# Four fp32 products over 392 columns made in three fp32r terms; the input splits shared out over ScalarE and GpSimd

## The chip, the cores and the metric

The kernel runs on one core of one Trainium2 chip. The metric is the time of one execution in device microseconds (us). Below this stands one time for each run, and one execution was also recorded by the hardware profiler.

Engines are named as the profile names them: PE is TensorE (its weight loads are PEld), DVE is VectorE, ACT is ScalarE, POOL is GpSimd, SP is SyncE, which issues the transfers. PSUM is the memory that the products write, in eight banks of 2 KB per partition; SBUF is the memory that all engines work from.

## The reference

Four attention blocks are applied in turn to 64 images of 256 channels and 14 x 14 = 196 tokens, all in float32.

```python
# block 0 (convolutional attention)
out = batchnorm1(x)
q, k, v = split(W_qkv_pw @ depthwise3x3(out))       # k, v resized to 7 x 7
o = softmax((q k^T + bias) * s) v                   # 4 heads
out = W_out_pw @ depthwise3x3(o) + x
x = W_mlp @ relu(batchnorm2(out)) + out
# block 1 (linear attention)
xn = group_norm(x, 8 groups);  k = softmax_channels(k);  q = softmax_tokens(q)
x = proj((q (k^T v))) + xn
# block 2 (8 heads)
hid = group_norm(x, 32 groups);  a = softmax(q k^T) v;  x = x + proj(a)
# block 3 (1 head)
xn = group_norm(x, 32 groups);   x = x + W_o (softmax(q k^T / 16) v)
```

## The kernel before

Images go through in 32 pairs. A pair's tensor has 128 partitions, 2 channel halves (c = 0, 1) and 392 columns (two images of 196 tokens). All four blocks of a pair stay on the chip; about five pairs are under way at once, each at another stage.

The order of the work is written out by hand in tables of numbers, one for each engine (PE_AT, ACT_AT, DVE_AT, POOL_AT, SP_AT). An entry such as `"kv0": 297` puts the piece kv0 of a pair in place 297 mod 128 of a loop body that has 128 places, 297 // 128 = 2 turns after the pair came in. One turn of the loop body (a period below) therefore does each piece once, for several pairs. Every engine works through its own list in order; semaphores tell it when inputs are there and when a buffer is free. A wait at the head of an engine's list holds all that stands behind it.

Names of pieces: q0, k0, v0, s0, t0, o0 are block 0's queries, keys, values, scores, transposes, output of attention; pw its second pointwise product (after the depthwise convolution conv2), mlp its last product; kv, q1, ctx, out belong to block 1; hq, hk, hv, sc, tn, av, rt, rep, proj to block 2 (sc scores, tn transposes, av values' products, rt and rep the denominators spread over the heads, proj the projection); v3, q3, s3, t3, o3 to block 3. gn1, gn2, gn3 are the group norms' products over groups.

A group norm goes like this: DVE takes statistics, PE averages over a group (a product over 8 columns), DVE copies the result (`gn_group`), GpSimd works out scale and shift in 20 small instructions on 4 elements (`normalized`, L561 to L585, with three Newton steps), and then writes the normalized input itself in 4 instructions over 196 columns (L590).

Products are of two kinds. `product` (L1168) multiplies in fp32: a product of 128 x 392 over 256 channels shows as 4 MATMUL records. `split_product` (L1174) takes inputs and weights that were split into two fp32r parts, high and low, and adds three terms (high x high, high x low, low x high) for each channel half: 6 records. For blocks 1, 2 and 3 the split of the normalized input is done each time by one ACT cast (the high part, L778) and one DVE subtraction (the low part, L1092) for each channel half, in buffers xs1, xs2, xs3. q0, pw, mlp and proj, two pieces each, are fp32 products of 392 columns.

The four banks ps_a, ps_b, ps_c, ps_e take turns by the table BANK_USES; the four banks of ps_s hold block 2's scores, their transposes, and the av products.

The depthwise convolutions are 2 + 16 DVE instructions each: k = 0 is a TENSOR_SCALAR for each half, k = 1 to 8 are SCALAR_TENSOR_TENSOR (`y = window * tap + y`, two inputs from SBUF), L1139 and L1158.

## Time and profile before

| | us |
|---|---|
| time, median of 3 runs | 2169.32 (2168.65 to 2169.71) |
| the profiled execution's own time | 2170.37 |
| its span, first to last instruction | 2168.3 |

| engine | busy us | share of the span | instructions |
|---|---|---|---|
| PE | 2076.3 | 96% | 15232 |
| PEld | 1686.7 | 78% | 15232 |
| DVE | 1820.4 | 84% | 4359 |
| ACT | 1527.8 | 70% | 5172 |
| POOL | 1278.3 | 59% | 2954 |

The busy time is that in which at least one instruction of the engine runs. ACT's instructions overlap, so the distance between two starts is less than a duration; the same holds for PE's, whose ends are modelled. The chain of waits that ended last lies on PE for 91% of the span, on DVE for 3%, on POOL for 2%.

### The profile page before, as it was taken

The page shows a single profiled execution, that of the slowest core. Times are in us where ns is not written, and L with a number is a line of the kernel's source. Part 1 is how long each engine was busy: PE and PEld are TensorE (multiplying, and loading weights), DVE is VectorE, ACT ScalarE, POOL GpSimd, SP SyncE. Part 2 cuts the span into 40 slices and gives each one's busy share as a digit, 9 for nine tenths or more (in the row PEclk, how much of TensorE's full clock was granted, in tenths as well). Part 3 has the DMA queues.
Part 4 walks back from the last instruction along what each step waited for, and adds up shares of the span by engine and source line. Part 5 has one row for each costly group of instructions (what it writes and reads, how often), then busy time and mean ns, then how long its engine had stood idle before and what let it go on. Part 6 is the DMA issues. An engine that isn't in the chain of part 4 may idle for free.

```text
span 2168.3 us, 58678 instructions
## 1 busy us (share of the span) xinstructions
PE 2076.3 (96%) x15232; PEld 1686.7 (78%) x15232; DVE 1820.4 (84%) x4359; ACT 1527.8 (70%) x5172; POOL 1278.3 (59%) x2954
## 2 busy tenths in 40 slices
PE   4679999999999999999999999999999999999987
PEld 3466888888888788888878888887888888788775
DVE  6778899988888998988899898888989888887532
ACT  2256777777777777777777777777777777777763
POOL 2455666666666666666666666666666666664311
PEclk8799999999999999999999999999999999999977
DMA  3000011001101100110110011011101100100000
GB/s 126 15 23 23 16 39 39 29 23 37 37 22 37 37 30 22 37 37 22 37 37 30 22 37 37 23 36 37 37 15 37 37 31 28 38 31 24 24 23 23
DMA packets 29828, 70.22 MB, mean 32 GB/s; under 512 B 6261, under 2 KB 7105, under 8 KB 29761
## 3 DMA queue, kind: packets, MB, share of 16 engines
q1 hardware_dynamic: 26928, 67.68, 9.0%
q10 hardware_dynamic: 2832, 1.73, 0.3%
q8 instruction: 32, 0.52, 0.1%
q14 instruction: 36, 0.29, 0.0%
HBM read 30.86 MB, written 12.85 MB: 20 GB/s over the span
## 4 chain that ended last, share of the span: by engine, by line
PE 91%; DVE 3%; POOL 2%; issue 2%; ACT 1%; SPq 1%; DMA 0%; POOLq 0%; DVEq 0%; ACTq 0%
PE ps_c L1166 19%; PE ps_a L1166 17%; PE ps_e L1166 17%; PE ps_b L1166 17%; PE ps_s L1166 10%; PE ps_s L1216 8%; POOL gn_t L579 1%; PE ps_a L1292 1%; DVE y L1158 1%; PE ps_e L1454 0%; PE ps_e L1292 0%; PE ps_b L1454 0%; PE ps_e L1399 0%; SPq L475 0%; ACT e L827 0%
## 5 line engine op out<-in xcount | busy, mean ns | idle before, releaser
L827 ACT ACTIVATE e<-ps_s,nm 98x196 f32<-98x196 f32 x1024 | 426.1, 446 | 89.9 <-DVE nm L956 89.8
L590 POOL TENSOR_SCALAR xn<-x,gn_scale,gn_shift 128x196 f32<-128x196 f32 x384 | 353.2, 933 | 20.8 <-POOL gn_shift L585 20.8
L1158 DVE SCALAR_TENSOR_TENSOR y<-opad,w_dw,y 128x406 f32<-128x406 f32 x512 | 301.8, 645 | 0.0
L1139 DVE SCALAR_TENSOR_TENSOR y<-xpad,w_dw,y 128x406 f32<-128x406 f32 x512 | 300.8, 640 | 0.0
L956 DVE TENSOR_REDUCE nm<-ps_s 98x4 f32<-98x784 f32 x256 | 240.6, 962 | 41.8 <-PE ps_s L1166 41.8
L834 ACT COPY pt<-ps_s 98x392 f32<-98x392 f32 x512 | 229.1, 503 | 42.6 <-PE ps_s L1216 41.8
L568 POOL TENSOR_TENSOR gn_t<-gn_group 128x4 f32<-128x4 f32 x96 | 34.3, 358 | 372.9 <-DVE gn_group L1006 286.5
L827 ACT ACTIVATION_READ_ACCUMULATOR e<-ps_s,nm 98x1 f32 x1024 | 231.6, 226 | 0.0
L1216 PE MATMUL ps_s<-w_eye,e 98*98 98x98 f32 x2048 | 204.6, 251 | 0.6 <-ACT e L827 0.6
L1216 PEld LDWEIGHTS ps_s<-w_eye,e 98*98 98x98 f32 x2048 | 186.3, 131 | 24.1 <-issue 16.2
L581 POOL TENSOR_SCALAR gn_t<-gn_t 128x4 f32<-128x4 f32 x288 | 119.7, 416 | 58.6 <-POOL gn_t L579 58.6
L1092 DVE TENSOR_TENSOR xs<-xn,xs 128x392 fp32r<-128x392 f32 x192 | 113.1, 589 | 41.7 <-ACT xs L778 39.3
L1166 PE MATMUL ps_a<-xs,ws_q 128*128 128x392 f32 x576 | 131.5, 363 | 0.4 <-ACT v L807 0.4
L1166 PE MATMUL ps_s<-k,q 32*98 32x196 f32 x2048 | 121.3, 352 | 8.6 <-ACT a L841 6.8
L778 ACT CAST xs<-xn 128x392 fp32r<-128x392 f32 x192 | 106.3, 554 | 31.4 <-POOL xn L590 31.3
L841 ACT COPY a<-ps_s 128x196 f32<-128x196 f32 x128 | 41.9, 327 | 119.2 <-PE ps_s L1166 113.5
L1166 PE MATMUL ps_s<-pt,v 98*32 98x196 f32 x2048 | 113.5, 339 | 3.5 <-ACT pt L834 2.7
L1166 PEld LDWEIGHTS ps_a<-xs,ws_q 128*128 128x128 f32 x576 | 102.0, 188 | 16.8 <-issue 7.7
L1166 PEld LDWEIGHTS ps_s<-k,q 32*98 32x98 f32 x2048 | 78.3, 163 | 46.8 <-issue 36.8
L937 DVE BATCH_NORM_STATS2 gn_stats<-x 128x6 f32<-128x196 f32 x384 | 110.4, 350 | 1.5
L579 POOL TENSOR_TENSOR gn_t<-gn_t,gn_half 128x4 f32<-128x4 f32 x288 | 95.7, 332 | 22.6
L578 POOL TENSOR_TENSOR gn_t<-gn_y 128x4 f32<-128x4 f32 x288 | 87.5, 304 | 23.1
(245 smaller groups left out, 5596.8 us busy)
## 6 DMA issues: line engine op xcount, KB each, us to landing
x_in<-in_x SPq DMA_DIRECT2D x32, 392.0 KB, 3.1
x_res<-in_x SPq DMA_DIRECT2D x32, 392.0 KB, 3.3
x2b<-x SPq DMA_DIRECT2D x32, 392.0 KB, 2.6
out<-x SPq DMA_DIRECT2D x32, 392.0 KB, 2.6
out_pairs<-out SPq DMA_DIRECT2D x32, 392.0 KB, 3.5
w_q<-in_q SPq DMA_DIRECT2D x3, 256.0 KB
w_k<-in_k SPq DMA_DIRECT2D x3, 256.0 KB
w_v<-in_v SPq DMA_DIRECT2D x3, 256.0 KB
```

The lines of the kernel that those rows point to most:

```text
L579: link(g.tensor_tensor(t.t[:], t.t[:], t.half[:], ALU.mult))
L581: link(g.tensor_scalar(t.t[:], t.t[:], 1.5, None, ALU.add))
L590: g.tensor_scalar(dst[:, c, of_image(i)], src[:, c, of_image(i)], t.scale[:, j:j + 1], t.shift[:, j:j + 1], ALU.mult, ALU.add).then_inc(t. ...
L827: s.activation(e2[:, j, tc], tile(use)[0:HALF, of_image(tc)], ACT.Exp, bias=nm2[:, j, tc:tc + 1], accum_out=den2[:, 2 * i + tc, h:h + 1]). ...
L834: s.copy(turned(j), tile(use)[0:HALF, 0:N2]).then_inc(emptied(use), 1)
L937: v.bn_stats(t.stats[:, j], src[:, j // 2, of_image(j % 2)]).then_inc(t.stat_steps.sem, 1)
L956: v.tensor_reduce(out=nm2[:, two], in_=ps_s[0:HALF, two, 0:N2].rearrange("p b (c n) -> p b c n", c=2), axis=AX.X, op=ALU.max, negate=True) ...
L1092: v.tensor_tensor(dst[:, 1, c], src[:, c], dst[:, 0, c], ALU.subtract).then_inc(gn[n].low.sem, 1)
L1139: v.scalar_tensor_tensor(out=dst, in0=window(xpad, c, k, CR), scalar=tap, in1=dst, op0=ALU.mult, op1=ALU.add).then_inc(conv1_steps.sem, 1)
L1158: v.scalar_tensor_tensor(out=dst, in0=window(opad, c, k, CR), scalar=tap, in1=dst, op0=ALU.mult, op1=ALU.add).then_inc(conv2_steps.sem, 1)
L1166: return nc.tensor.matmul(dst, lhsT, rhs, start=start, stop=stop)
L1216: last = nc.tensor.transpose(tile(use)[0:HALF, of_tile(sc, tc)], e2[:, j, tc, sc * HALF:(sc + 1) * HALF], eye[0:HALF, 0:HALF])
```

## The change

- q0, pw, mlp and proj become `split_product`s: 6 records in place of 4 for each of the 8 pieces of a pair. Their weights are split once at the start.
- Their inputs are split each time, for each channel half by an ACT cast and a GpSimd subtraction: y1 (for q0) and an2 (for proj) into a buffer xs_a, y2 (for pw) and act0 (for mlp) into a buffer xs_b. xs_a also takes the place of rt2, act0 now lies in y2's memory, an2 in a2's.
- The normalized input of the three group norms is written by ACT (4 instructions of 128 x 196 each), no longer by GpSimd.
- The low parts for blocks 1, 2 and 3 are subtracted by GpSimd, no longer by DVE.
- The av products go to ps_a and ps_e and ps_c, out of ps_s.
- All tables of order and BANK_USES are new, and what PE folds of the weights at the start is spread over the first pair's stages.

```diff
 POOL_AT = {
-    "resize0": 0, "resize1": 16, "probs0": 64, "probs1": 96, "gn1": 240, "gn2": 304, "gn3": 544, "rows3": 592,
+    "resize0": 87, "y1_low0": 93, "y1_low1": 98, "resize1": 104, "probs0": 168, "probs1": 180, "y2_low0": 244,
...
-                for c in range(KC):
-                    for i in range(2):
-                        j = 2 * c + i
-                        alone()
-                        g.tensor_scalar(dst[:, c, of_image(i)], src[:, c, of_image(i)], t.scale[:, j:j + 1],
-                                        t.shift[:, j:j + 1], ALU.mult, ALU.add).then_inc(t.done.sem, 1)
...
+                    for n, src, dst, _ in splits:
+                        for c in range(KC):
+                            p = pair_of(t, u, POOL_AT[f"low{n}_{c}"])
+                            if p is not None:
+
+                                pool.wait_ge(gn[n].high.sem, gn[n].high.at(p, c + 1))
+                                g.tensor_tensor(dst[:, 1, c], src[:, c], dst[:, 0, c], ALU.subtract).then_inc(gn[n].low.sem, 1)
+
+                    for c in range(KC):
+                        p = pair_of(t, u, POOL_AT[f"y1_low{c}"])
+                        if p is not None:
+                            pool.wait_ge(y1_cast.sem, y1_cast.at(p, c + 1))
+                            g.tensor_tensor(by_image(xs_a[:, 1, c]), conv_tokens(y1, c), by_image(xs_a[:, 0, c]),
+                                            ALU.subtract).then_inc(y1_cut.sem, 1)
...
+                    for n, src, dst in ((1, x1, xn1), (2, x2, xn2), (3, x3, xn3)):
+                        for c in range(KC):
+                            p = pair_of(t, u, ACT_AT[f"norm{n}_{c}"])
+                            if p is not None:
+                                act.wait_ge(gn[n].steps.sem, gn[n].steps.at(p + 1, 0))
+                                if n == 1 and has_before(p):
+                                    act.wait_ge(*read(p - 1, f"out{c}"))
...
+                                for i in range(2):
+                                    j = 2 * c + i
+                                    s.activation(dst[:, c, of_image(i)], src[:, c, of_image(i)], ACT.Identity,
+                                                 scale=gn[n].scale[:, j:j + 1], bias=gn[n].shift[:, j:j + 1]
+                                                 ).then_inc(gn[n].done.sem, 1)
...
+                            act.wait_ge(*read(p, f"rep{c}"))
+                            act.wait_ge(*full(p, latest("rep0", "rep1")))
+                            s.copy(by_image(xs_a[:, 0, c]), an2[:, :, c]).then_inc(an2_cast.sem, 1)
...
-                            for source in elsewhere(use, "rep0", "rep1"):
-                                pe.wait_ge(*read(p, source))
-                            product(tile(use)[:, 0:N2], lambda k: w["p2"][:, k, of_chunk(c)], lambda k: an2[:, :, k]
-                                    ).then_inc(filled(use), 1)
-
+                            pe.wait_ge(an2_cut.sem, an2_cut.at(p, KC))
+                            split_product(tile(use)[:, 0:N2], lambda a, k: ws["p2"][:, a, k, of_chunk(c)],
+                                          lambda b, k: xs_a[:, b, k]).then_inc(filled(use), 1)
```

Three places in the new order matter for what follows. The first is GpSimd behind block 1's group norm (the piece gn1), before the change:

```order
L584 TENSOR_TENSOR gn_t<-gn_group,gn_scale 128x4
L585 TENSOR_TENSOR gn_shift<-w_gn_b,gn_t 128x4
L590 TENSOR_SCALAR xn<-x,gn_scale,gn_shift 128x196 x4
L547 TENSOR_TENSOR rs_d<-y 128x168
L548 TENSOR_TENSOR rs_d<-rs_d,w_frac 128x168
```

And the same place after it:

```order
L618 TENSOR_TENSOR gn_t<-gn_group,gn_scale 128x4
L619 TENSOR_TENSOR gn_shift<-w_gn_b,gn_t 128x4
L687 TENSOR_TENSOR xs_a<-a,xs_a 128x392 x2
L664 TENSOR_TENSOR xs<-xn,xs 128x392 x2
L581 TENSOR_TENSOR rs_d<-y 128x168
```

The four instructions on xn are gone; in their place stand the low parts of proj's input and of block 1's input, four subtractions that each wait for a cast by ACT.

The second place is DVE behind the copy of the same group norm's result (`gn_group`). The y rows are block 0's first convolution, nm the score maxima of block 2, m, t, nm (98x2) those of block 3. Before the change:

```order
L1006 COPY gn_group<-ps_b 128x8
L1063 TENSOR_TENSOR rt<-ps_e,rt 8x392
L1139 SCALAR_TENSOR_TENSOR y<-xpad,w_dw,y 128x406 x2
L956 TENSOR_REDUCE nm<-ps_s 98x4 x2
L1139 SCALAR_TENSOR_TENSOR y<-xpad,w_dw,y 128x406 x2
L1103 TENSOR_REDUCE m<-ps_e 98x2
L1105 TENSOR_TENSOR t<-m,rb 98x2
L1106 SCALAR_TENSOR_TENSOR nm<-t,rs 98x2
L1139 SCALAR_TENSOR_TENSOR y<-xpad,w_dw,y 128x406 x4
```

After it:

```order
L1104 COPY gn_group<-ps_e 128x8
L1221 SCALAR_TENSOR_TENSOR y<-xpad,w_dw,y 128x406 x2
L1158 TENSOR_TENSOR xs_a<-ps_a,xs_a 8x392
L1054 TENSOR_REDUCE nm<-ps_s 98x4 x2
L1186 TENSOR_REDUCE m<-ps_a 98x2
L1188 TENSOR_TENSOR t<-m,rb 98x2
L1189 SCALAR_TENSOR_TENSOR nm<-t,rs 98x2
L1221 SCALAR_TENSOR_TENSOR y<-xpad,w_dw,y 128x406 x8
L1166 TENSOR_TENSOR a<-ps_e,a 128x2x196
L1221 SCALAR_TENSOR_TENSOR y<-xpad,w_dw,y 128x406 x2
```

The convolution's instructions stood in groups of 2, 2 and 4; now eight stand in a row, while GpSimd works on this group norm.

The third place is ACT around the casts for block 1 (`xs`). opad is block 0's attention output, a that of block 2. Before the change:

```order
L834 COPY pt<-ps_s 98x392 x2
L778 CAST xs<-xn 128x392
L725 COPY opad<-ps_b 128x14x14 x2
L788 ACTIVATE q<-ps_a,qb2s 128x392
L778 CAST xs<-xn 128x392
L725 COPY opad<-ps_c 128x14x14 x2
```

After it:

```order
L932 COPY pt<-ps_s 98x392 x2
L871 CAST xs_a<-a 128x392
L840 ACTIVATE xn<-x,gn_shift,gn_scale 128x196 x4
L879 CAST xs<-xn 128x392
L780 COPY opad<-ps_b 128x14x14 x2
L879 CAST xs<-xn 128x392
L780 COPY opad<-ps_c 128x14x14 x2
```

ACT now waits here for GpSimd's scale and shift before four instructions on xn, and the copies to opad, from which conv2 starts, stand behind them.

## Rows read from the trace of the kernel before

**Rows 1.** Stretches: busy us (count) of each engine, clock, DMA share, GB/s

```profile
600.00:1230.60 630.60, 629.90 (x4741) 515.18 (x4740) 565.69 (x1350) 473.29 (x1611) 405.85 (x921) 1.00 0.09 32
240.00:2020.00 1780.00, 1777.59 (x13401) 1455.04 (x13395) 1580.02 (x3781) 1335.45 (x4545) 1133.09 (x2594) 1.00 0.09 32
```

**Rows 2.** Timeline of PE: start us, us, line, operation, out<-in, records merged

```profile
1001.11 1.24 PE L1166 MATMUL ps_a<-xs,ws_q 128*128 128x392 f32 x6
1002.18 1.48 PE L1166 MATMUL ps_c<-act,w_mlp 128*128 128x392 f32 x4
1003.50 1.48 PE L1166 MATMUL ps_b<-act,w_mlp 128*128 128x392 f32 x4
...
1010.24 0.28 PE L1166 MATMUL ps_b<-gn_mine,w_group 128*128 128x8 f32 x2
...
1022.04 1.35 PE L1166 MATMUL ps_a<-xs,ws_q 128*128 128x392 f32 x6
1023.23 0.82 PE L1166 MATMUL ps_b<-pt,v 128*128 128x196 f32 x4
...
1026.77 1.58 PE L1166 MATMUL ps_b<-an,w_p 128*128 128x392 f32 x4
1028.28 0.92 PE L1166 MATMUL ps_s<-k,q 32*98 32x196 f32 x16
1029.13 1.62 PE L1166 MATMUL ps_c<-ws_kv,xs 128*98 128x512 f32 x6
...
1632.82 1.48 PE L1166 MATMUL ps_c<-act,w_mlp 128*128 128x392 f32 x4
```

**Rows 3.** Timeline of ACT, same columns

```profile
1027.56 1.15 ACT L875 ACTIVATE e<-e,r 98x196 f32<-98x196 f32 x3
...
1056.22 0.54 ACT L778 CAST xs<-xn 128x392 fp32r<-128x392 f32 x1
1056.63 0.75 ACT L673 ACTIVATE xpad<-x_in,bn_shift,bn_scale 128x392 f32<-128x392 f32 x1
```

**Rows 4.** Groups by line: busy us, mean ns, idle before and releaser

```profile
L1092 DVE TENSOR_TENSOR xs<-xn,xs 128x392 fp32r<-128x392 f32 x192 | 113.1, 589 | 41.7 <-ACT xs L778 39.3
L590 POOL TENSOR_SCALAR xn<-x,gn_scale,gn_shift 128x196 f32<-128x196 f32 x384 | 353.2, 933 | 20.8 <-POOL gn_shift L585 20.8
```

**Rows 5.** POOL's instructions on tile p: duration ns min/median/max

```profile
L602 POOL TENSOR_TENSOR p<-s,r x64: 840/846/1182, 47.2 to 1954.6; 98x392 f32<-98x392 f32 x64
```

**Rows 6.** Waits of POOL from 600 to 1230.6 us: total, times, longest

```profile
POOL gn_t L568 <- DVE gn_group L1006: 91.7, 30, 4.7
POOL rb L615 <- ACT v3t L850: 34.6, 10, 3.5
...
POOL p L602 <- DVE r L979: 4.1, 10, 0.4
```

**Rows 7.** Timeline of DVE: convolution steps in a row

```profile
137.68 5.60 DVE L1139 SCALAR_TENSOR_TENSOR y<-xpad,w_dw,y 128x406 f32<-128x406 f32 x10
...
1045.85 4.50 DVE L1158 SCALAR_TENSOR_TENSOR y<-opad,w_dw,y 128x406 f32<-128x406 f32 x8
...
1080.09 2.30 DVE L1139 SCALAR_TENSOR_TENSOR y<-xpad,w_dw,y 128x406 f32<-128x406 f32 x4
```

**Rows 8.** Timeline of POOL in the same places, and one group norm at the end

```profile
137.10 6.24 POOL L579 TENSOR_TENSOR gn_t<-gn_t,gn_half 128x4 f32<-128x4 f32 x1
...
1045.22 5.51 POOL L590 TENSOR_SCALAR xn<-x,gn_scale,gn_shift 128x196 f32<-128x196 f32 x1 [0.22 <-POOL gn_shift L585]
...
1080.89 0.45 POOL L582 TENSOR_TENSOR gn_y<-gn_y,gn_t 128x4 f32<-128x4 f32 x1
...
2090.72 0.20 POOL L568 TENSOR_TENSOR gn_t<-gn_group 128x4 f32<-128x4 f32 x1 [22.78 <-PE ps_c L1166]
...
2097.28 1.98 POOL L590 TENSOR_SCALAR xn<-x,gn_scale,gn_shift 128x196 f32<-128x196 f32 x4 [0.22 <-POOL gn_shift L585]
```

**Rows 9.** Waits of ACT from 600 to 1230.6 us: total, times, longest

```profile
ACT a L841 <- PE ps_s L1166: 35.6, 20, 3.2
```

**Rows 10.** Timeline of PE in the first pair's stages

```profile
67.12 2.95 PE L1166 MATMUL ps_e<-y,w_o 128*128 128x392 f32 x4 [8.70 <-DVE y L1158]
```

More of the change, by code:

```diff
@@ L320, in latest, with earliest, ahead @@
             return max(names, key=filled_at)
+        def earliest(*names):
+            return min(names, key=filled_at)
+        def ahead(use, other):
+            return (PE_AT[use] - 1 - PE_AT[other]) // SLOTS
         def comes_after(use, older):
@@ new lines, in step @@
+                    for c in range(KC):
+                        p = pair_of(t, u, ACT_AT[f"y1_high{c}"])
+                        if p is not None:
+                            act.wait_ge(conv1_steps.sem, conv1_steps.at(p, KC * 8 + c + 1))
+                            older = p + ahead(earliest("q0_0", "q0_1"), latest("proj0", "proj1"))
+                            if exists(older):
+                                act.wait_ge(*full(older, latest("proj0", "proj1")))
+                            if has_before(p):
+                                act.wait_ge(*full(p - 1, latest("q0_0", "q0_1")))
+                            s.copy(by_image(xs_a[:, 0, c]), conv_tokens(y1, c)).then_inc(y1_cast.sem, 1)
@@ new lines, in step @@
+                    for c in range(KC):
+                        p = pair_of(t, u, ACT_AT[f"y2_high{c}"])
+                        if p is not None:
+                            act.wait_ge(conv2_steps.sem, conv2_steps.at(p, KC * 8 + c + 1))
+                            if has_before(p):
+                                act.wait_ge(*full(p - 1, latest("mlp0", "mlp1")))
+                            s.copy(by_image(xs_b[:, 0, c]), conv_tokens(y2, c)).then_inc(y2_cast.sem, 1)
+                    for c in range(KC):
+                        p = pair_of(t, u, ACT_AT[f"act0_high{c}"])
+                        if p is not None:
+                            act.wait_ge(act0_done.sem, act0_done.at(p, c + 1))
+                            act.wait_ge(*full(p, latest("pw0", "pw1")))
+                            s.copy(xs_b[:, 0, c], act0[:, c]).then_inc(act0_cast.sem, 1)
```

213 lines of the change are left out of this document (133 added, 80 removed), and 69 rows, old and new, of tables (ACT_AT, BANK_USES, DVE_AT, PE_AT).

## The prediction, made before the changed kernel ran

> **What bounds the kernel now.** I read the busy time by stretch first. From 240 to 2020 us PE is busy 1777.6 of 1780 us at a granted clock of 1.00 [rows 1]: 2.4 us of idle time in 1780. So between these marks the time is what PE's records take one after the other, and the other engines matter only when one holds PE up. The same mlp piece starts at 1002.18 and, ten periods on, at 1632.82 [rows 2], so a period is 63.06 us, and the stretch holds 28.2 of them. Per period (630.6 us is ten) DVE is busy 56.6, ACT 47.3, POOL 40.6 us [rows 1]. POOL's figure is too small: most of its instructions wait for the one ahead on POOL itself. Its waits for others are 9.2 + 3.5 + 0.4 = 13.0 us a period [rows 6], so 50.0 of 63.06 are taken. The remaining 390 us, filling and draining, have PE partly idle, as in the 8.70 us before pw of the first pair [rows 10].
>
> **PE.** Distances from start to start count, not durations. An fp32 piece over 392 columns takes 1003.50 - 1002.18 = 1.32 us, and 1.51 us at the costlier place (1026.77 to 1028.28); three terms take 1.07 (1001.11 to 1002.18) to 1.19 us (1022.04 to 1023.23) [rows 2]. As most fp32 pieces are at 1.32 and few above, I take 1.34 against 1.10: 0.24 a piece, times 8 = 1.9 us a period. Bounds: 8 x (1.32 - 1.19) = 1.0, and 2.3 if the fp32r pieces are all at 1.07 and two fp32 pieces at about 1.5. PE alone then needs 63.06 - 1.9 = 61.15 us. The av products keep their form; another bank changes no PE time, and only frees the first score bank earlier. The wider weights are split at the start, beside the fp32 folding that now leaves PE's front.
>
> **ACT.** Added: 8 casts, whose distance is 0.41 us (1056.22 to 1056.63), 3.3 us; and 12 instructions of 196 columns from SBUF. The nearest is e<-e,r, three in 1.15 us with a last one of about 0.45: 0.35 each, 4.2 us [rows 3]. ACT gets 47.3 + 7.5 = 54.8 us of 61.2. This hides beside PE if ACT's forced waits stay under 6.4 us; before, it had 15.7 us to spare, most of it harmless waiting ahead of PE (the largest, for av, 3.6 us a period [rows 9]).
>
> **DVE.** Six subtractions go, 6 x 0.589 = 3.5 us [rows 4]: 53.1 us. None was waited for by PE, so nothing comes from it but room.
>
> **POOL.** Twelve instructions on xn go: 353.2 / 32 = 11.0 us a period [rows 4]. Fourteen subtractions over 392 columns come. The only one of this size on POOL takes 0.846 us, 1.182 at most [rows 5]: 14 x 0.85 = 11.9 us, at most 16.5. 50.0 - 11.0 + 11.9 = 50.9 us of 61.2. That looks free, but the 0.93 us mean of the removed ones [rows 4] tells of something else: alone they take 0.5 (four in 1.98 us, [rows 8]), and one took 5.51 us. It lies under eight convolution steps of DVE in a row (1045.85, 4.50 us); an instruction of four elements took 6.24 us under ten (137.68, 5.60 us); under four steps at 1080.09 one took 0.45 us [rows 7, 8]. So POOL, when caught at the start of such a row, stands until the row ends, and DVE is not slowed (0.55 us a step each time).
>
> The Trainium skill, SBUF — State Buffer, on engine ports, calls the shared pair an exclusive lock that goes to whichever of the two engines starts first, the loser being fully blocked. Full blocking agrees with the 5.51 us; that the first one wins does not, as POOL's instruction started at 1045.22, before DVE's row. What it would make of the time is the last rival.
>
> The new order puts eight steps in a row on DVE just when POOL works on gn1, and leaves eight in a row under gn3. Where the blocked work used to be xn of a norm that had time, it now lies inside a chain that PE waits for. Between gn1's product and kv0, PE now has about 18.9 us of other work (1010.24 to 1029.13, [rows 2]), and by the same distances about 17.7 us for the 19 pieces that stand there after the change. The chain in that gap: DVE copy 0.3, POOL's 20 instructions 6.55 (2090.72 to 2097.28, [rows 8]), four xn on ACT 1.4, cast 0.4, opad copies 0.4, cast 0.4, last subtraction 0.85: 10.3 us undisturbed. Fully blocked by all 14 steps in that stretch, 14 x 0.55 = 7.7, it is 18.0 us and kv0 is late by some 0.3, or by 1.1 if a subtraction is at its 1.18 and the an2 pair is in its way: about 0.7. If POOL slips in between the steps, nothing is late. gn3, followed by y2's subtractions and pw, has the same form: 0 to 0.7. Bounds 0 to 1.35 a period; two of the three rows of steps above blocked POOL fully, but chains have to be wholly blocked to be late at all, so I take 0.35. Period: 61.5 us.
>
> **Ends.** In filling, block 0 of the first pair is a chain. Three splits come into it, each cast 0.42, subtraction 0.85 twice, about 2.1 us, against three times 0.5 from the products; some 13 us of folding leave PE's front but the weights' casts come before ACT's first split. In draining, one split (2.1) and slower subtractions add to the last pair, ACT's faster xn takes away. I take +2 us in all, -8 to +10.
>
> **The sum.** Against the profiled execution's own 2170.4 us (span 2168.3 and 2.1 around it): 2170.4 - 28.2 x 1.9 (53.9) + 28.2 x 0.35 (9.9) + 2 = 2128.4. The median of the runs lies 1.1 lower than that execution, so 2127.
>
> **The rivals.**
> 1. POOL's blocking decides. Both chains are late in full, 1.35 a period: 62.5 us, 2170.4 - 53.9 + 38.1 + 2 - 1.1 = 2155. For it: rows 7 and 8, and that POOL's 50.9 us plus two fully blocked rows of eight (8.8) make 59.7 of 61.2, so that a delay cannot be made up. Against: before, norms under such steps did not hold PE.
> 2. ACT becomes the bound, and the kernel slower. xn on ACT stands at the head of its list behind POOL. Where gn1, gn2 or gn3 ends 3 us after ACT gets there, ACT stands three times 3 us; with 54.8 of work that is 63.8 us, 0.75 over the old period: 2169.3 + 28.2 x 0.75 + 2 = 2192. It decides from 8.3 us of forced waits on (63.06 - 54.8). For it: the blocked chains, and opad and score work queued behind xn. Against: ACT waited 15.7 us a period before and PE lost nothing.
> 3. Three terms are not cheaper by what I say: 1.0 a period with the same 0.35 of waits, 62.4: 2169.3 - 18.3 + 2 = 2153. For it: 1.19 stands beside 1.07 in rows 2. Against: most pieces there are near 1.1.
> 4. DVE's convolution steps wait behind POOL's subtractions, 14 x 0.85 = 11.9: 53.1 + 11.9 = 65.0 us, 2169.3 + 28.2 x 1.94 + 2 = 2226. The steps' even 0.55 us beside a busy POOL speaks against it [rows 7]. This is what the lock rule of the SBUF page would give.
>
> **How the numbers follow.** Forecast 0.50, rival 1 0.22, rival 2 0.15, rival 3 0.10, rival 4 0.03. What a measurement can tell from no change is 0.2%, 4.3 us. Rivals 1 and 3 lie 14 to 16 us under the old time with a spread of about 12, so a tenth of them ends inside 0.2% and a little beyond; of rival 2 some is inside as well. Faster 0.77, same 0.06, slower 0.17. The forecast's own range is 2106 to 2148: a saving of 2.3 without waits and with good ends at the low end (2170.4 - 64.9 + 0 - 1.1 = 2104), 1.4 with 0.7 of waits at the other. The range over all cases reaches up through rivals 1 and 3 and the lower part of rival 2: 2105 to 2176.
>
> **What would show it.** Between 240 and 2000 us a period of 61.2 to 61.8 us, pieces of six records 1.07 to 1.19 us apart, PE idle under 1 us a period and that before kv or pw. Rival 1: PE idle 1 us or more a period before kv, proj or pw, released by POOL, and POOL instructions of 4 to 6 us inside the norms. Rival 2: ACT's waits for gn_shift over 5 us a period. Rival 3: distances of 1.2 us and a full PE. Rival 4: convolution steps over 0.55 us apart. Wrong altogether would be a PE with idle time before other pieces than these, for the tables move all of them.

## The result, and the profile of the changed kernel

The changed kernel takes 2231.11 us (median of 4 runs, 2227.89 to 2235.72) against 2169.44 of the kernel before on the same chip (2168.65 to 2169.71): a ratio of 1.0284, 95% interval 1.0272 to 1.0297. It is 61.7 us slower, where 42 us faster was forecast.

A period is read here, in every kernel, as the mean distance of the same product over 20 pairs in the middle: the first one that uses a pair's contexts in block 1 (`qe,cx`, the piece out). The time from the start to the first such product is called below the beginning, and what follows it the steady part. It was 63.06 us and is 65.05 (441.74 to 1742.67 us: 1300.93 / 20). From the first such product to the last, 31 pairs on, it is 1936.1 us before and 1985.3 after, 49.1 more; what lies ahead of the first (111.9, now 129.3) and behind the last (120.3, now 115.4) is 12.5 more. Together these are the 61.6 by which the span grew (2168.3 to 2229.9).

Ten periods of the changed kernel by stretch (busy us and count of each engine, then the granted clock, DMA share, GB/s), to be held against [rows 1]:

```profile
600.00:1250.00 650.00, 623.05 (x4938) 545.48 (x4941) 565.95 (x1297) 557.95 (x1815) 425.05 (x942) 1.00 0.09 32
```

PE is idle for 27 of 650 us, where it was idle for 0.7 before. Its work per period has gone down as meant (62.4 us busy, 63.0 before), so that is not where the time went. PE had 91% of the chain that ended last before; the shares are now:

```profile
PE 59%; DVE 15%; issue 11%; ACT 8%; POOL 5%; DVEq 1%; ACTq 1%; POOLq 0%
```

The bound has passed to a chain through several engines, DVE first. PE's longest waits (total, times, longest, in the same ten periods) say where:

```profile
PE ps_c L1545 <- DVE kv L1113: 12.5, 10, 1.3
PE ps_e L1545 <- DVE kv L1113: 5.7, 10, 0.6
```

Both are the transposes of kv, which wait for DVE. The timelines of DVE, POOL and PE at that place (start us, us, line, operation, out<-in, records merged, idle time before):

```profile
1012.96 2.53 DVE L1240 SCALAR_TENSOR_TENSOR y<-opad,w_dw,y 128x406 f32<-128x406 f32 x2
1015.41 0.68 DVE L1113 TENSOR_TENSOR kv<-ps_c,w_kvb 98x512 f32<-98x512 f32 x1
...
1012.84 2.22 POOL L670 TENSOR_TENSOR xs_a<-y,xs_a 128x392 fp32r<-128x392 f32 x2 [0.80 <-ACT xs_a L852]
...
1016.22 0.54 PE L1545 MATMUL ps_c<-w_eye,e 98*98 98x98 f32 x4 [1.26 <-DVE kv L1113]
1017.33 0.54 PE L1545 MATMUL ps_e<-w_eye,e 98*98 98x98 f32 x4 [0.57 <-DVE kv L1113]
```

Two convolution steps take 2.53 us in place of some 1.2 (four took 2.30 in [rows 7]), beside the 2.22 us in which POOL makes y1's low parts. kv stands behind them, and PE behind kv. Over the whole kernel such steps (busy, mean ns) take 739 and 674 ns in the mean, 645 and some 640 in the kernel before:

```profile
L1240 DVE SCALAR_TENSOR_TENSOR y<-opad,w_dw,y 128x406 f32<-128x406 f32 x512 | 349.3, 739 | 0.0
L1221 DVE SCALAR_TENSOR_TENSOR y<-xpad,w_dw,y 128x406 f32<-128x406 f32 x512 | 315.8, 674 | 0.0
```

A second thing is new, where DVE's loop turns round. The last instruction of one period, the first of the next, and the wait in ten periods:

```profile
1034.24 0.16 DVE L1043 TENSOR_TENSOR gn_mine<-gn_mine,gn_sq 128x4 f32<-128x4 f32 x1
1037.47 0.75 DVE L1203 SCALAR_TENSOR_TENSOR out<-ps_a,ob,out 128x196 f32<-128x196 f32 x2 [3.06 <-issue]
```

```profile
DVE out L1203 <- issue: 29.9, 10, 3.2
```

"issue" names no releaser. From the start of the loop's branch to the start of the loop's first instruction DVE takes 2.81 us in the median of the periods, where the kernel before took 0.32. (The 0.13 of the expectations below is the distance to a DVE instruction that had been issued ahead of the branch.) What else happens there is in the part of the page on DMA queues (packets, MB, share), where the queue that reads instructions has 158 packets of 8 KB, 5 of them in each period inside the loop:

```profile
q14 instruction: 158, 1.29, 0.2%
```

The same row of the kernel before had 36, none inside the loop:

```profile
q14 instruction: 36, 0.29, 0.0%
```

### The profile page after: what moved, and what is told of

Read it like the earlier page. It is cut to its first block, busy times and chain, and to the rows that moved or that the text cites. A ratio compares the mean times of both kernels' runs of the same rounds, so it can differ in the third digit from the quotient of the medians.

```text
span 2229.9 us, 60029 instructions
## 1 busy us (share of the span) xinstructions
PE 2048.8 (92%) x15744; PEld 1788.9 (80%) x15744; DVE 1814.4 (81%) x4175; ACT 1794.9 (80%) x5820; POOL 1370.3 (61%) x3018
## 4 chain that ended last, share of the span: by engine, by line
PE 59%; DVE 15%; issue 11%; ACT 8%; POOL 5%; DVEq 1%; ACTq 1%; POOLq 0%
PE ps_c L1248 15%; PE ps_a L1248 14%; PE ps_b L1248 13%; PE ps_e L1248 6%; PE ps_s L1304 6%; DVE y L1240 5%; PE ps_s L1248 3%; ACT e L925 3%; DVE kv L1113 2%; DVE y L1221 2%; ACT y L793 1%; ACT xn L840 1%; POOL gn_t L615 1%; PE ps_e L1545 1%; ACT v3t L947 1%
## 5 line engine op out<-in xcount | busy, mean ns | idle before, releaser
L664 POOL TENSOR_TENSOR xs<-xn,xs 128x392 fp32r<-128x392 f32 x192 | 194.6, 1029 | 121.7 <-ACT xs L879 121.7
L840 ACT ACTIVATE xn<-x,gn_shift,gn_scale 128x196 f32<-128x196 f32 x384 | 187.3, 576 | 24.8 <-POOL gn_shift L619 24.4
L1248 PE MATMUL ps_b<-xs,ws_q 128*128 128x392 f32 x768 | 165.7, 351 | 0.0
L1248 PEld LDWEIGHTS ps_b<-xs,ws_q 128*128 128x128 f32 x768 | 139.5, 191 | 5.0
L615 POOL TENSOR_SCALAR gn_t<-gn_t 128x4 f32<-128x4 f32 x288 | 105.2, 365 | 56.4 <-POOL gn_t L613 56.4
L1248 PE MATMUL ps_c<-xs_a,ws_q 128*128 128x392 f32 x384 | 91.5, 375 | 41.9 <-POOL xs_a L670 40.7
L799 ACT ACTIVATE kv<-kv,nmk 98x256 f32<-98x256 f32 x128 | 69.0, 539 | 68.6 <-DVE nmk L1115 68.4
L1248 PE MATMUL ps_c<-ws_v,xs 128*98 128x256 f32 (+1 forms) x768 | 116.6, 294 | 6.4 <-POOL xs L664 6.4
L687 POOL TENSOR_TENSOR xs_a<-a,xs_a 128x392 fp32r<-128x392 f32 x64 | 77.0, 1206 | 72.9 <-ACT xs_a L871 72.9
L1248 PEld LDWEIGHTS ps_c<-ws_v,xs 128*98 128x98 f32 x768 | 95.7, 166 | 17.7 <-issue 17.6
L1248 PE MATMUL ps_e<-ws_kv,xs 128*98 128x512 f32 x384 | 102.4, 402 | 6.7 <-POOL xs L664 6.7
```

The lines of the kernel that those rows point to most:

```text
L615: link(g.tensor_scalar(t.t[:], t.t[:], 1.5, None, ALU.add))
L664: g.tensor_tensor(dst[:, 1, c], src[:, c], dst[:, 0, c], ALU.subtract).then_inc(gn[n].low.sem, 1)
L687: g.tensor_tensor(by_image(xs_a[:, 1, c]), an2[:, :, c], by_image(xs_a[:, 0, c]), ALU.subtract).then_inc(an2_cut.sem, 1)
L840: s.activation(dst[:, c, of_image(i)], src[:, c, of_image(i)], ACT.Identity, scale=gn[n].scale[:, j:j + 1], bias=gn[n].shift[:, j:j + 1]). ...
L1248: return nc.tensor.matmul(dst, lhsT, rhs, start=start, stop=stop)
```

## The experiments

Two suspects, then. **A**: DVE's loop is read again at each turn, because its 301 instructions (counted in the program as built) lie over one block of code more than the engine holds. **B**: POOL's two-input subtractions slow DVE's convolution steps; at one place (B1) or all over (B2). **C** is the prediction's rival 2, ACT and the chains of waits. All ratios are to the kernel before on the same chip. The edits follow below the table.

| kernel | us | ratio, 95% | period | PE busy per period |
|---|---|---|---|---|
| kernel before | 2169.4 | | 63.06 | 62.99 |
| changed kernel | 2231.1 | 1.0272 to 1.0297 | 65.05 | 62.37 |
| pad100 | 2232.4 | 1.0275 to 1.0303 | 64.90 | 62.86 |
| small_lows | 2159.4 | 0.9928 to 0.9958 | 62.49 | 61.64 |
| one_term | 2226.8 | 1.0219 to 1.0276 | 65.58 | 59.27 |
| before_pad170 | 2200.3 | 1.0117 to 1.0148 | 64.21 | 63.48 |
| y1_small | 2186.4 | 1.0061 to 1.0092 | 63.24 | 61.79 |
| late_y1 | 2206.6 | 1.0153 to 1.0181 | 63.71 | 61.89 |
| late_pad | 2182.3 | 1.0037 to 1.0064 | 62.62 | 61.51 |
| copy_lows | 2192.3 | 1.0081 to 1.0111 | 63.18 | 61.74 |
| q0_fp32 | 2196.0 | 1.0101 to 1.0132 | 63.93 | 62.39 |
| q0_fp32_pad | 2180.2 | 1.0032 to 1.0060 | 63.13 | 62.00 |
| fp32_small | 2189.8 | 1.0071 to 1.0103 | 63.11 | 63.04 |
| late_pad_first | 2179.5 | 1.0032 to 1.0064 | 62.74 | 61.51 |
| kv_first | 2184.6 | 1.0057 to 1.0083 | 62.97 | 61.80 |
| kv_first_pad | 2160.9 | 0.9951 to 0.9977 | 61.95 | 61.42 |
| kv_late_first | 2174.0 | 1.0010 to 1.0038 | 62.51 | 61.42 |
| late_pad256 | 2221.7 | 1.0229 to 1.0258 | 63.70 | 61.91 |

**Is it DVE's loop turn, POOL, or a chain?**

```diff
+            for _ in range(100):
+                dve.sem_inc(dve_held, 1)
             dve.wait_ge(first_in, FIRST)
```

> The changed kernel with 100 one-number semaphore increments on VectorE ahead of its first wait; nothing in the loop is touched, only where its code lies moves. Theory A (VectorE's loop body is read again from memory at each turn, because it lies over one block of code more than the engine holds): the gap behind the loop branch falls from 2.81 us to about 0.13, the reads on the instruction queue inside the loop go away, and the period falls from 65.05 us by 1.0 to 2.7; time 2155 to 2203 us, against 2231 of the changed kernel. Theory B (VectorE's convolution steps are slowed by GpSimd's two-input subtractions) and theory C (ScalarE's and GpSimd's chains of waits): the gap may go, but its time comes back as another wait; time 2225 to 2233.

2232.4 us: no gain, though all that A says of the turn came true: the gap is 0.27 us, the reads fell from 158 to 42. So as a cause by itself A fails here. Where the time came back can be read off. Undisturbed periods are 63.5 us, one less than the 64.55 of the changed kernel; but in most periods (65.1) PE's clock falls behind its wait for kv (16 such stretches in the 20 periods in the middle). The timeline of PE, and below it stretches of 2 us:

```profile
1017.91 0.54 PE L1547 MATMUL ps_c<-w_eye,e 98*98 98x98 f32 x4 [1.23 <-DVE kv L1115]
1019.02 0.58 PE L1547 MATMUL ps_e<-w_eye,e 98*98 98x98 f32 x4 [0.57 <-DVE kv L1115]
```

```profile
1016.00:1018.00 2.00, 0.77 (x5) 0.45 (x4) 1.97 (x3) 0.00 (x0) 1.92 (x3) 1.00 0.52 201
1018.00:1020.00 2.00, 1.43 (x12) 1.23 (x13) 1.93 (x6) 1.34 (x4) 1.56 (x5) 0.85 0.00 0
1020.00:1022.00 2.00, 2.00 (x12) 1.86 (x11) 1.85 (x11) 1.50 (x5) 0.55 (x2) 0.50 0.00 0
1022.00:1024.00 2.00, 2.00 (x9) 1.52 (x9) 1.36 (x4) 2.00 (x9) 0.00 (x0) 0.80 0.00 0
```

Here the clock is at the lower of its two levels, 1.2 GHz (0.50), for some 3 us behind two waits that make 1.8 us of idle time within 3, and the period is 1.6 us longer. Such waits don't decide it by themselves: in the changed kernel PE has the same two in every period, and only 5 of 20 periods show the drop (66.15 us against 64.55). Why more of them have it in pad100 is not shown. In the kernels below whose waits for kv are shorter, none of the periods in the middle has one.

```diff
-  g.tensor_tensor(dst[:, 1, c], src[:, c], dst[:, 0, c], ALU.subtract).then_inc(gn[n].low.sem, 1)
+  cols = slice(0, N2 if is_first(p) else 8)
+  g.tensor_tensor(dst[:, 1, c, cols], src[:, c, cols], dst[:, 0, c, cols], ALU.subtract).then_inc(gn[n].low.sem, 1)
   ... (and the same for y1, y2, act0 and an2)
```

> The changed kernel with GpSimd's 14 subtractions per pair cut to 8 columns (every instruction and wait stays; the first pair is left whole), so that the low parts are not all computed. Theory B: the convolution steps fall from 739 and 674 ns back to 645 and 640 and the period falls by 1 to 2.5 us; time 2160 to 2203. Theory A: the gap of 2.81 us behind VectorE's branch stays and decides; the period falls by under 0.7 us; time 2211 to 2231. Theory C: ScalarE's chain keeps its length, time over 2225.

2159.4 us, a little below what B expected (2160 to 2203), with the gap of 2.8 us still there. POOL has 12 us a period less, but DVE also has 3.0 us less (56.4 to 53.4), and the same place now reads:

```profile
981.62 1.19 DVE L1245 SCALAR_TENSOR_TENSOR y<-opad,w_dw,y 128x406 f32<-128x406 f32 x2
982.73 0.69 DVE L1118 TENSOR_TENSOR kv<-ps_c,w_kvb 98x512 f32<-98x512 f32 x1
```

1.19 us for the two steps, and no wait of PE for kv. B holds. ACT alone, as in rival 2, is out: it is as busy as before (55.7 us). But POOL's part in a chain got shorter here as well, so this run doesn't rule out that POOL itself was late; kv_first below, where POOL keeps all its work, does.

```diff
-  split_product(tile(use)[:, 0:N2], lambda a, k: ws["q0"][:, a, k, of_chunk(c)],
+  eight_product(tile(use)[:, 0:N2], lambda a, k: ws["q0"][:, a, k, of_chunk(c)],   # high by high only
   ... (and the same for o0, mlp0 and p2)
```

> The changed kernel with TensorE's eight split products in one term (high by high, 2 records of 6) instead of three: 32 records fewer per pair of images, some 32 x 0.17 = 5.5 us of a period of 65.05. If TensorE's work sets the period, the period falls by 4 us or more and the time is below 2120 us. Theories A, B and C (a chain through VectorE, with or without its gap, holds TensorE up): part of it turns into idle time of TensorE; VectorE busy 56.4 + gap 2.8 = 59.2 us is the floor; time 2120 to 2200.

2226.8 us, outside the range. PE is busy 6% less (585.8 us in 650, from 623.1) and 4 us come of it. PE does not set the pace in the changed kernel; its waits are for DVE:

```profile
PE ps_a L1248 <- DVE out L1203: 18.7, 10, 2.1
PE ps_c L1550 <- DVE kv L1113: 14.2, 10, 1.4
```

The first is what stands behind the loop's turn, the second behind the slow steps. The upper bound expected, 2200, took the 59.2 us of DVE's work and gap as the floor; the period is 65.58. PE waits longer in the same places, and its clock drops more often (0.97 in this stretch).

**The kernel before, with its loop moved.**

```diff
+            for _ in range(170):
+                dve.sem_inc(dve_held, 1)
```

> The kernel before with 170 such increments ahead of VectorE's first wait. Theory A: its loop body, too, now lies over one block more, the gap behind its branch grows from 0.13 us to about 2.8, five reads per period show on the instruction queue, and the time grows; TensorE has only 63.06 us of work per period and VectorE more room than in the changed kernel, so by 0.3 to 2.5 us per period, 2178 to 2240 us. If theory A is wrong on what makes the gap (another property of the changed kernel's loop), the gap stays at 0.13 us and the time at 2169 plus at most 1 us for the increments.

2200.3 us, +30, inside A's range. Nothing of the loop was touched. Its wait in ten periods, and its row of instruction reads:

```profile
DVE xs L1094 <- issue: 23.1, 10, 2.5
```

```profile
q14 instruction: 157, 1.29, 0.2%
```

157 reads for 36, a wait without a releaser of 2.3 us, and 1.15 us more per period. From the branch to the loop's first instruction it is 2.82 us, from 0.32. So A is a true cost of where the loop's code lies, worth 30 us in a kernel bound by PE; in the changed kernel it lay beside a larger one.

**One place or all fourteen?**

```diff
-  g.tensor_tensor(by_image(xs_a[:, 1, c]), conv_tokens(y1, c), by_image(xs_a[:, 0, c]), ALU.subtract)
+  cols = slice(0, TOK if is_first(p) else 4)
+  g.tensor_tensor(by_image(xs_a[:, 1, c])[:, :, cols], conv_tokens(y1, c)[:, :, cols], by_image(xs_a[:, 0, c])[:, :, cols], ALU.subtract)
```

> The changed kernel with only the two subtractions of y1's low part (2 of GpSimd's 14 per pair) cut to 8 columns, so that those low parts are not all computed. Theory B1, one place decides: these two run beside two of VectorE's second-convolution steps, which take 1280 and 1329 ns there against 640 elsewhere, and VectorE's kv behind them is what TensorE waits 1.26 us for. The two steps fall to about 640 each, the waits of TensorE at the transposes of kv (1.26 and 0.57 us) go, and with them most of the clock drops: period 62.5 to 63.4 against 65.05, time 2160 to 2185. Theory B2, all fourteen count alike (VectorE's 3.0 us of slowing, GpSimd's 12 us of work): two of fourteen give 0.3 to 0.5 us per period, time 2217 to 2224. Theory C (ScalarE's chain): over 2225.

2186.4 us (1.4 above B1's range): two of the fourteen subtractions carry 45 of the 72 us of small_lows. Of PE's two waits for kv the second is left:

```profile
PE ps_e L1546 <- DVE kv L1114: 6.3, 11, 0.6
```

**The same subtractions at another place of POOL's order.**

```diff
-    "resize0": 87, "y1_low0": 93, "y1_low1": 98, "resize1": 104,
+    "resize0": 87, "y1_low0": 105, "y1_low1": 106, "resize1": 104,
```

> The whole computation of the changed kernel; the two subtractions of y1's low part are issued behind the second image's resizing on GpSimd, not ahead of it (slots 105 and 106 for 93 and 98). By theory B1 they then run beside VectorE's kv, nmk and nmq instructions or in GpSimd's pause of 3 us behind the resizing (1018.9 to 1021.9 us), 3 us before TensorE's q product needs them (1024.7). The resizing comes beside the two convolution steps instead (its first instructions make such a step 0.9 us, not 1.3): TensorE's wait falls from 1.83 to 0.5 us or so; period 63.0 to 64.0; time 2172 to 2203. By B2 the slowing is only moved: 2222 to 2235.

2206.6 us: 24.5 us gained, 3.6 above the upper bound expected. The subtractions now run beside reductions and kv, but the resizing has come beside the two steps, and these take 1.61 us there, so half of the wait stays.

With 100 increments on top:

> late_y1 with the 100 semaphore increments ahead of VectorE's first wait, so that VectorE's loop code is not read again at each turn. By theory A with B1 (the gap of 2.81 us costs 1.0 us per period once the clock drops are gone, as the undisturbed periods of the two kernels show, 64.55 and 63.55): 0.3 to 1.0 us per period below late_y1, 8 to 28 us; 2150 to 2190. If the gap costs nothing (theory A wrong for this kernel): the time of late_y1 within 4 us.

2182.3, 24 us less again, in range. With PE's wait smaller and the clock drops gone, the turn of the loop is worth 0.9 to 1.1 us a period, as A said.

**The form of POOL's instruction.**

```diff
-  g.tensor_tensor(dst[:, 1, c], src[:, c], dst[:, 0, c], ALU.subtract).then_inc(gn[n].low.sem, 1)
+  alone()
+  g.tensor_scalar(dst[:, 1, c], src[:, c], 1.0, None, ALU.mult).then_inc(gn[n].low.sem, 1)
   ... (and the same for the other four)
```

> The changed kernel with GpSimd's 14 subtractions per pair turned into one-input multiplications by 1.0 of the same size (the low parts are then not computed: the output of these products is another), each behind one semaphore increment that takes the wait. Theory B, two-input form on GpSimd slows VectorE's steps: the steps beside them take 630 to 645 ns as those beside the one-input scaling of the kernel before did, although GpSimd is as busy as now; period 62.5 to 63.5, time 2160 to 2190. Rival: any GpSimd work of a microsecond on these tiles slows the steps, or GpSimd's own queue is what is late: the steps stay at 1.3 us or the time over 2215.

2192.3 us, just above the range. Beside the an2 parts the steps (L1223 here) take 634 to 636 ns in the mean, where the subtractions made them 732 in the mean and 936 at most. Two steps and POOL's instruction there, in the changed kernel and in this one:

```profile
1001.99 1.48 DVE L1221 SCALAR_TENSOR_TENSOR y<-xpad,w_dw,y 128x406 f32<-128x406 f32 x2
1001.34 1.14 POOL L687 TENSOR_TENSOR xs_a<-a,xs_a 128x392 fp32r<-128x392 f32 x1 [1.39 <-ACT xs_a L871]
...
984.86 1.18 DVE L1223 SCALAR_TENSOR_TENSOR y<-xpad,w_dw,y 128x406 f32<-128x406 f32 x2
984.29 1.24 POOL L690 TENSOR_SCALAR xs_a<-a 128x392 fp32r<-128x392 f32 x1 [1.50 <-ACT xs_a L873]
```

POOL starts first in both, so at this place it is the form that makes the difference. Between 300 and 1900 us the 23 steps of the changed kernel that begin while a subtraction runs take 0.93 us each, and the 46 that were ahead of one keep 0.63; in copy_lows it is 0.63 either way, but for one case of 0.73 in 50. Beside the y1 parts there is still some slowing:

```profile
995.51 1.44 DVE L1242 SCALAR_TENSOR_TENSOR y<-opad,w_dw,y 128x406 f32<-128x406 f32 x2
...
995.82 2.54 POOL L672 TENSOR_SCALAR xs_a<-y 128x392 fp32r<-128x392 f32 x2 [0.31 <-ACT xs_a L854]
```

1.44 us, between 1.19 and 2.53. POOL is a little busier than in the changed kernel (45 us of 65, 42.5 there), so the amount of its work is not the point; the two-input form is most of it. As DVE's pair starts first here, and POOL's in the changed kernel, this run does not tell form from order of start at this second place, and the step that begins while POOL's one-input instruction runs takes 0.89 us even so.

**One product given back.** The casts and subtractions of y1 are left out as well:

```diff
-  pe.wait_ge(y1_cut.sem, y1_cut.at(p, KC))
-  split_product(tile(use)[:, 0:N2], lambda a, k: ws["q0"][:, a, k, of_chunk(c)], lambda b, k: xs_a[:, b, k])
+  pe.wait_ge(conv1_steps.sem, conv1_steps.at(p, KC * 9))
+  product(tile(use)[:, 0:N2], lambda k: ws["q0"][:, 0, k, of_chunk(c)].bitcast(F32),
+          lambda k: y1[:, k].rearrange("p (i r) n -> p i (r n)", i=2)[:, :, 0:TOK])
```

> The changed kernel with one of its four products, q0, back in fp32: y1's casts and subtractions are gone, TensorE reads y1 itself and, for weights, the high parts taken as fp32 numbers (the low part of these weights is then left out). By theory B1 the two slow convolution steps go, as in y1_small (63.24 us per period); TensorE has two of its eight dear products back, by the saving that the kernels show so far (63.06 against 61.64 us busy, 1.4 for eight) 0.35 us more; 63.2 to 63.9 per period, and q0 of the first pair no longer waits for low parts, so 0 to 6 us off the beginning: 2180 to 2203. By B2 (all fourteen subtractions alike) 2215 to 2228.

> q0_fp32 with the 100 semaphore increments ahead of VectorE's first wait. Theory A: VectorE's gap of 2.81 us per turn goes; TensorE's work (62.0 us) and the one wait of 0.57 us per period then set the pace, 62.3 to 62.9 us: 2158 to 2182 us, below late_pad (2182) if the beginning is shorter too. If the gap is hidden here: the time of q0_fp32 within 4 us. It is the candidate for a kernel that beats the one before (2170).

2196.0 and 2180.2 us, both in range, but by a balance: the periods, 63.93 and 63.13, lie above theirs, and the beginning is shorter than expected. The period is 0.69 us above that of y1_small (0.35 was expected for the terms), and the steady part begins at 117.5 us, 11.8 before the changed kernel's. The pad brings 16 us, 0.8 a period.

**The price of the form.** small_lows, and in its eight pieces:

```diff
-  split_product(...)
+  for k in range(KC):
+      ins = mm(dst, lhsT(0, k).bitcast(F32), rhs(0, k).bitcast(F32), k == 0, k == KC - 1)
```

> small_lows (2159 us, period 62.49, TensorE 61.64 us busy) with TensorE's eight split products made of fp32 products of the high parts instead (the low parts are left out), 4 records for 6. With GpSimd's subtractions out of the way TensorE sets the pace, so this is the price of the form: if three fp32r terms are cheaper by the 1.4 us per period that 63.06 - 61.64 shows, 63.3 to 64.2 per period and 2183 to 2205 us; by the prediction's 1.9, up to 2212; by its rival 3 (three terms are not cheaper) 2150 to 2163.

2189.8 us. PE is full:

```profile
600.00:1250.00 650.00, 649.17 (x4876) 531.79 (x4876) 551.76 (x1325) 574.14 (x1877) 311.75 (x969) 1.00 0.09 32
```

63.04 us of work per period against 61.64: three terms save 1.40 us for eight pieces. That they are not cheaper at all is out. The forecast's 1.9 and rival 3's 1.0 miss by about as much, and 1.40 lies inside the bounds of 1.0 to 2.3.

**The beginning.** late_pad, and for q0:

```diff
   if is_first(p):
-      pe.wait_ge(early_steps, loaded_by("q0"))
+      pe.wait_ge(conv1_steps.sem, conv1_steps.at(p, KC * 9))
+      product(tile(use)[:, 0:N2], lambda k: w["q0"][:, k, of_chunk(c)], lambda k: y1[:, k] ...)
+  else:
```

> The whole computation: late_pad (2182) with q0 of the first pair of images alone computed in fp32 from y1 itself, all later pairs in three terms. Theory on the ends: the first pair's q0 waits 35 us for y1's low parts behind GpSimd's first resizing and for the split weights, and the pipeline fills later for it; q0_fp32 began its steady part at 117.5 us, the changed kernel at 129.3 and late_pad at 134. With the period of late_pad kept (62.62 us), 10 to 16 us are to be had: 2166 to 2173, equal to the kernel before (2170) or a little under it. If the beginning is late for another reason (the eight more weight splits on ScalarE and VectorE, the other order of slots): 2178 to 2184.

The time is above the range of the theory (2166 to 2173) and in that of its rival (2178 to 2184). Yet the beginning is shorter: the steady part begins at 123.6 us and not at 134.1, and the profiled execution is 8.8 us shorter (2174.0 to 2182.8). But the times lie in two groups, 2174 to 2176 and 2183 to 2185, with a median of 2179.5, so of the 10 us only 3 show in it. The second group is not explained.

**Only the order of kv and the steps on DVE.** This changes one number:

```diff
-    "conv2_1": 195, "conv2_2": 201, "conv2_3": 207, "conv2_4": 221,
+    "conv2_1": 195, "conv2_2": 201, "conv2_3": 218, "conv2_4": 221,
```

> The whole computation of the changed kernel, with one slot number changed on VectorE: the pair of steps of the second convolution that stands ahead of the second kv product (conv2_3, slot 207) is issued behind it and the next (slot 218). Theory B1 says that TensorE's 1.26 us come from these two steps' length (1280 and 1329 ns beside GpSimd's subtractions) because kv stands behind them. Out of the way, they may stay slow where they now run: TensorE's waits of 1.26 and 0.57 us go, period 63.2 to 64.1 against 65.05, 2178 to 2205 us. If VectorE's total slowing of 3.0 us per period is what costs, wherever it falls: over 2222.

2184.6 us, in range: 46.5 us from it, as much as from taking the work away in y1_small. The period, 62.97, is a little below its range, and the steps that moved did not stay slow. POOL's pair now runs beside kv itself, and the moved pair behind it:

```profile
993.84 0.68 DVE L1113 TENSOR_TENSOR kv<-ps_c,w_kvb 98x512 f32<-98x512 f32 x1
996.87 1.43 DVE L1240 SCALAR_TENSOR_TENSOR y<-opad,w_dw,y 128x406 f32<-128x406 f32 x2
...
993.73 1.89 POOL L670 TENSOR_TENSOR xs_a<-y,xs_a 128x392 fp32r<-128x392 f32 x2 [0.81 <-ACT xs_a L852]
```

kv, with one input out of PSUM, takes its 0.68 us beside it, and the two steps 1.43 in place of 2.53. So one number did two things: it took kv out from behind the steps, and the steps out from beside the subtractions; DVE is busy 55.1 us a period, from 56.4. POOL has the same work, so POOL itself was not what came late. And with 100 increments:

> kv_first with the 100 semaphore increments ahead of VectorE's first wait. Theory A: the turn-around of VectorE's loop costs 0.9 us per period where TensorE waits behind it, as late_y1 to late_pad showed (24 us): 2155 to 2182. If moving the steps has given VectorE the room to hide it: the time of kv_first within 5 us.

2160.9 us, ratio 0.9964 (0.9951 to 0.9977): the only whole computation here that beats the kernel before, by 0.4%. Its stretch of 650 us, the waits of PE that are listed for it, and the turn of DVE's loop:

```profile
600.00:1250.00 650.00, 644.59 (x5130) 568.94 (x5129) 583.62 (x1359) 582.61 (x1907) 435.67 (x984) 1.00 0.09 32
```

```profile
PE ps_b L1250 <- DVE gn_mine L1045: 2.5, 11, 0.3
PE ps_a L1250 <- DVE xs_a L1160: 2.2, 10, 0.2
```

```profile
1003.20 0.16 DVE L1045 TENSOR_TENSOR gn_mine<-gn_mine,gn_sq 128x4 f32<-128x4 f32 x1
1004.36 0.75 DVE L1205 SCALAR_TENSOR_TENSOR out<-ps_a,ob,out 128x196 f32<-128x196 f32 x2 [1.00 <-PE ps_a L1250]
```

PE is idle for 5.4 of 650 us, and DVE's first work after the turn waits for PE again, not PE for it.

All repairs together:

> All the repairs together, the whole computation: conv2_3 behind the second kv, y1's subtractions behind the resizing, 100 increments, q0 of the first pair in fp32. TensorE's work is 61.5 us per period and late_pad's waits at the transposes of kv (0.30 and 0.57 us) should go: 61.7 to 62.2 us per period, ends as late_pad_first: 2145 to 2165, below the kernel before (2170). If the waits come back elsewhere in the chain through VectorE: 2166 to 2180.

2174.0 us (12 runs, 2167.1 to 2182.1): worse than kv_first_pad, and in the range given for waits that come back elsewhere. The period is 62.51 against 61.95 with the same work on PE, and DVE is 0.7 us busier per period (56.1 to 55.4). The trace shows where:

```profile
994.54 1.90 DVE L1244 SCALAR_TENSOR_TENSOR y<-opad,w_dw,y 128x406 f32<-128x406 f32 x2
...
994.70 2.55 POOL L670 TENSOR_TENSOR xs_a<-y,xs_a 128x392 fp32r<-128x392 f32 x2 [0.17 <-POOL yr L593]
```

```profile
PE ps_b L1252 <- DVE gn_mine L1045: 7.6, 11, 0.7
```

The later subtractions meet the moved steps again: 1.90 us for the pair, 1.43 in kv_first. Behind these steps stand the statistics of a group norm, and PE's product over groups now waits 7.6 us in ten periods for them, where it waited 2.5. That is 0.5 of the 0.56 us lost a period. The two repairs of one collision get in each other's way. The beginning is not shorter either: the steady part starts at 131.3 us, though the first q0 is as early as in late_pad_first; why is not shown.

**Control for A**, late_y1 with 256 increments:

> Control for theory A: late_y1 with 256 increments instead of the 100 of late_pad. If it is the place of the loop's code in blocks of 256 instructions that counts, the place is again that of late_y1: the gap is 2.8 us again, five reads per period, 2203 to 2210 us. If any increments ahead of the loop help (by shifting the engines in time): 2180 to 2186 as late_pad.

Its wait at the turn of the loop, in ten periods:

```profile
DVE out L1205 <- issue: 30.2, 10, 3.2
```

The gap (2.80 us), the reads (159, 157 in late_y1) and late_y1's period (63.70 to 63.71) are back. The time is 2221.7 and not 2206, because with 256 increments the steady part begins at 148.9 us in place of 132.6; that was left out of the expectation. So the place modulo 256 instructions counts, not a shift in time. The other kernels fit: with none or 256 increments ahead of the changed loop there is the gap, with 100 there is not.

## Why the prediction was wrong

- **PE, "0.24 a piece, times 8 = 1.9".** Right in kind, too large: 1.40 (fp32_small against small_lows), which is inside its bounds. 0.5 us a period, 14 us in all.
- **ACT, 54.8 us.** Measured 55.7; it is hidden. In kv_first_pad ACT does the same work in a period of 61.95. Rival 2 did not come true.
- **DVE, "nothing comes from it but room", and "DVE is not slowed".** This is the step that failed, and most of the miss. 53.1 us were forecast, 56.4 came; without the subtractions 53.4. The even 0.55 us a step in [rows 7] was measured beside a POOL that scaled with one input and stood still [rows 8]. The other rows there had POOL instructions of 4 elements beside them. All this was carried over to subtractions of 392 columns with two inputs, which the trace did not show beside such steps. But it did show smaller ones. In the kernel before, two steps take 1.36 us where two instructions of the resizing over 84 columns, with two inputs each, lie beside them, and 1.19 where only instructions of 4 elements do (at 1039.33):

```profile
1027.62 1.36 DVE L1158 SCALAR_TENSOR_TENSOR y<-opad,w_dw,y 128x406 f32<-128x406 f32 x2
...
1027.53 0.35 POOL L553 TENSOR_TENSOR rs_e<-rs_e,w_frac 128x84 f32<-128x84 f32 x1
1028.06 0.47 POOL L557 TENSOR_TENSOR yr<-rs_x,rs_e 128x84 f32<-128x84 f32 x1 [0.18 <-POOL rs_e L553]
```

So "DVE is not slowed" was read from three places of the trace and a fourth spoke against it. The Trainium skill, SBUF — State Buffer, says that a DVE instruction with two inputs in SBUF and a GpSimd instruction that reads SBUF exclude each other, and that the one that starts first gets the ports. The rows agree for the steps (1.2 us a pair, 2.53 beside POOL) and for kv, which has one input in PSUM and kept its 0.68 us. That the first one wins holds for the subtractions (at 1012.84 us, and in all 69 steps beside the an2 parts). It does not hold for the one-input scaling at 1045.22 in [rows 8], nor for the one-input multiplications of copy_lows beside the an2 parts, which started first and slowed no step but one in 50. One input is no safeguard either: beside the y1 parts such a multiplication slowed the step behind its start to 0.89 us.
- **Rival 4** was given 3 in 100, and its 65.0 us a period and 2226 us are almost what was measured, by another way: it charged all 14 subtractions to DVE's total work. DVE is not full. Two subtractions at one place ahead of kv cost 45 us; the other twelve, with their work on POOL, the remaining 27 of small_lows. That 2226 is near the time is luck.
- **Waits, 0.35 us with bounds 0 to 1.35.** Measured 65.05 - 61.95 = 3.1 us more than in kv_first_pad: 2.08 by the order of kv and the steps, clock drops included (kv_first), and 1.02 by the turn of the loop (its pad). The shares hold for this sequence only: with the pad first it is 0.15 for the turn (pad100) and 2.95 for the order. Together they are what is shown. In kv_first_pad 0.5 of idle time is left. The prediction looked for late chains behind POOL in the group norms; the late one was a DVE instruction queued behind two others that a POOL instruction slowed. Rival 1 is wrong.
- **The turn of DVE's loop** was in no term. The Trainium skill, Runtime: NRT & Kernel Launch, Instruction fetch mechanics, says that most engines hold two blocks of 256 instructions and that a taken branch to a place outside them waits for a read. The traces agree: 11 of the 18 kernels have the gap of 2.8 us and 157 to 159 reads, the other 7 have 0.3 us and 36 or 42. DVE's loop has 301 instructions (311 before), so by that rule it fits two blocks or spans three by where it starts; the start-up code ahead of it went from 752 to 926 instructions (counted in the programs as built). That the third block is the cause is inferred from the rule; the runs show that the place modulo 256 decides.
- **Ends, "+2, -8 to +10".** 12.5 us: 17.4 later at the first context product, 4.9 less behind the last. q0_fp32 takes 11.8 of the 17.4 back, so most of it is the first pair's q0, which waits for split y1. PE's first instruction, and the first q0 of the kernel before:

```profile
35.30 2.30 PE L1248 MATMUL ps_c<-xs_a,ws_q 128*128 128x392 f32 x6 [35.30 <-POOL xs_a L670]
...
20.18 3.78 PE L1166 MATMUL ps_s<-w_p,w_v 128*128 128x256 f32 x8 [20.18 <-DMA w_qb_rep<-in_qb_rep]
...
33.17 2.96 PE L1166 MATMUL ps_c<-y,w_q 128*128 128x392 f32 x4
```

The first q0 starts 2.1 us later than before, as costed. But before, PE folded weights from 20.18 us until then; now it stands, and the folding comes between later links of the chain (40.30 to 68.8 us). Had q0 not waited for split y1, it would have started 11 us earlier (24.39 in q0_fp32). The prediction saw the folding leave PE's front and priced only the splits.

Sum: 0.5 + 2.08 + 1.02 = 3.6 us a period, against 65.05 - 61.5 = 3.55 missed. Over 28.2 periods this is 100 us, and 10.5 at the ends make 110.6, 6.5 more than the miss of 104: near both ends the periods grew by less than in the middle, so that first to last product is 49.1 us longer and not 28.2 x 1.99 = 56.1.

The prediction's own arithmetic is off in two small places: 28.2 x 1.9 is 53.6 and not 53.9, and the low end is worked out as 2104 where the ranges begin at 2106 and 2105.

Not settled: why PE's clock drops in some periods of the changed kernel and not in others, the two groups of times of late_pad_first, and why a one-input instruction of POOL slows a step at the y1 place and not beside the an2 parts. DVE's gap was removed only by moving the code, not by a loop of under 256 instructions.

## What to carry to other kernels

An operation moved to GpSimd is costed not only there: list the VectorE instructions that run beside it, ask which of them have two inputs in SBUF, and what is queued behind them that TensorE waits for. Such a collision need not be paid for by giving the work back: one slot number, which parted the two and freed what was queued behind, gave 46.5 of the 62 us lost. Check then what the moved work meets at its new place, as kv_late_first shows. Before comparing two versions of a kernel with a loop, look at the wait without a releaser at the loop's turn and at the instruction reads: code ahead of the loop alone moved a kernel by 24 to 30 us.
